# A transformer block pair on one core: the tokens of a batch dealt to four tiles in turn

## The chip, the cores and the metric

One core of a Trainium2 chip runs the whole kernel; the other seven are idle. The core has TensorE (matmuls into PSUM, and their weight loads), VectorE, ScalarE and GpSimd, which read and write SBUF with 128 partitions, and DMA queues. The metric is device time in microseconds of one execution.

## The reference

`x` has 8 batches (B) of 512 tokens (S) with 256 features (D). Two layers follow each other, each adding its result to `x`:

```
x = x + bitlinear(gelu(bitlinear(adapter(x, language))))       # layer 0
x = x + bitlinear(silu(conv3(bitlinear(subject_linear(x)))))   # layer 1

adapter:        h = x + relu(x @ W1[id] + b1[id]) @ W2[id] + b2[id]; layer norm, gamma[id], beta[id]
subject_linear: x @ W[id].T + bias[id]
bitlinear:      weights rounded to -1, 0, 1 times one scale;
                each token rounded to 8 bits by its own largest absolute value; matmul (256 -> 1024 or back)
conv3:          per channel (1024), 3 taps along the 512 tokens of a batch, zero at both ends
```

Everything but `conv3` treats each token by itself. `conv3` needs the tokens of a batch side by side, in their order.

## The kernel before

A batch has TB = 4 tiles of P = 128 tokens. In token layout a partition holds one token of each tile: `xs`, the running value of `x`, keeps on partition p the tokens p, 128 + p, 256 + p and 384 + p, each with 256 features (1 KB). In channel layout a partition is a feature, and the 512 tokens lie along it.

Every engine has one queue with a written order. In `first()` single steps are listed by hand (layer 0 for all batches and the start of layer 1), then `slot2(s)` runs for s = 3 to 8 with the steps of several batches interleaved, then `ending()`. Engines wait for one another through semaphores. A slot of layer 1 moves one batch on by one stage.

The steps that matter here:

- `load_first_tokens` and `load_tokens` (ScalarE's queue) load `xs` of a batch through `x_tiles`; `store2` (SyncE's queue) stores one tile of the result through `out_tiles`.
- `adapter_out(b, p)` (TensorE, L1310): for two tiles, `hT`, the hidden values of the adapter in channel layout, is the stationary operand, 128 tokens at a time; `cw2` is the moving one. It leaves token layout in PSUM.
- `transpose_x` (L1379), `linear` (L1401, L1404) bring a batch through the subject's matrix; `absmax_y`, `scale_y`, `inverse_y` (VectorE) and `round_y` (ScalarE, L619) round it; `transpose_y` (L1416) brings it to channel layout in PSUM, and `lead_q` (ScalarE, L626) copies it into `yT`, bf16, [128, 2, 512].
- `spread_scales` (L1424) and `lead_scales` (ScalarE, L636): the scale of each token, spread to all partitions, is copied from PSUM into `dqb`, [128, 512] fp32.
- `up(b, f)` (L1437): the block f of 128 hidden channels, two matmuls with ternary weights stationary and the 512 columns of `yT` moving. A batch has 8 of them, all batches 64.
- `dequant` (VectorE, L1113) multiplies by `dqb` into `apad`; `last_tap` (ScalarE, L645), `first_tap` (VectorE, L1120), `middle_tap` (GpSimd, L886) and `tap_sum` (GpSimd, L893) make the convolution in `conv`, which is kept in the memory `raw_all`.
- `transpose_conv(b, k)` (L1458): eight transposes of 128 tokens by 128 channels back to token layout. The data are the stationary operand, an identity the moving one. `silu` (ScalarE, L656), the rounding (`round2`), a DMA transpose and `down2` (L1481, L1482) follow.

Of the kernel before, what the change touches and what calls it, by code (L numbers as in the profile page):

```python
# [7 lines left out]
ACT = mybir.ActivationFunctionType  # L8
# [7 lines left out]
P = 128  # L16
# [12 lines left out]
def build_program(nc, t):  # L29
    B, S, D = t["x"].shape  # L30
# [4 lines left out]
    KD = D // P  # L35
    KH = H // P
    TB = S // P
# [6 lines left out]
    with ExitStack() as ctx:  # L44
        def sb(name, shape, dt=F32):
            return ctx.enter_context(nc.sbuf_tensor(name, shape, dt))

        def sem(name):
            return ctx.enter_context(nc.semaphore(name))
# [4 lines left out]
        def wait(eng, s, n):  # L54

            if isinstance(n, int) and n <= 0:
                return
            eng.wait_ge(s, n)
# [3 lines left out]
        def bank(k, n=1):  # L62
            return psum[:, k, :] if n == 1 else psum[:, k:k + n, :]
# [5 lines left out]
        id32 = sb("id32", [P, P])  # L69
# [31 lines left out]
        cw2 = [sb(f"cw2_{k}", [A + 1, D]) for k in range(2)]  # L101
# [5 lines left out]
        dqb = [sb(f"dqb{k}", [P, S]) for k in range(2)]  # L107
        mid_all = [sb(f"mid{k}", [P, 2 * S + 1]) for k in range(2)]
        hT = sb("hT", [A + 1, S])
# [43 lines left out]
        def bank_adapted(b, p):  # L153
            if b == 0:
                return BANK_UP + p
            if b == 1 and p == 1:
                return BANK_UP + 2
            return BANK_AD
# [85 lines left out]
        yT = [sb(f"yT{k}", [P, KD, S], BF16) for k in range(2)]  # L244

        apad = sb("apad", [P, KH, SP2])
        conv = [raw_all[:, 2 * k:2 * k + 2, :].rearrange("p a (f s) -> p (a f) s", s=S) for k in range(2)]
# [17 lines left out]
        def bank_c(b, k):  # L265
            return 3 if b == B - 1 and k % 2 == 1 else 5
# [8 lines left out]
        def bank_x(b):  # L275
            return 0
# [26 lines left out]
        p_bce = sem("p_bce")  # L303
# [44 lines left out]
        def tile(b, j):  # L348
            return TB * b + j + 1

        def pair(b, p):
            return PAIR * b + p + 1
# [9 lines left out]
                slot2(s)  # L362
            ending()

        x_tiles = t["x"].rearrange("b (t p) d -> b p t d", p=P)
        xT_tiles = t["xT"].rearrange("(k p) (b s) -> b p k s", p=P, b=B)
        cw1_all = t["cw1"].rearrange("l (k p) a -> l p k a", p=P)
        out_tiles = t["out"].rearrange("b (t p) d -> b t p d", p=P)
        wl_all = t["cwl1"].rearrange("l (k p) o -> l p k o", p=P)

        block = ctx.enter_context(nc.Block())
# [114 lines left out]
        def _(act):  # L486
# [142 lines left out]
            def lead_scales(b):  # L629
                act.wait_ge(p_bc, b + 1)  # L630
                if b == 0:

                    act.wait_ge(s_zg, PAIRS)
                    act.wait_ge(s_ssq, PAIRS)
                wait(act, p_a, KH * (b - 1))
                act.activation(dqb[b % 2][:, :], bank(bank_x(b)), ACT.Copy).then_inc(p_bce, 1)  # L636

            def last_tap(b, f):

# [46 lines left out]
            def slot2(s):  # L686
                on(last_tap, s - 1, 2)
                on(last_tap, s - 1, 3)
                on(silu, s - 2, 0)
                on(last_tap, s - 1, 4)  # L690
                on(round2, s - 3, 3)
                on(last_tap, s - 1, 5)
                on(silu, s - 2, 1)
                on(dequant2, s - 3, 1)
                on(round_y, s, 0)
                on(round_y, s, 1)
                on(last_tap, s - 1, 6)
                on(round2, s - 2, 0)
                on(lead_scales, s)
                on(last_tap, s - 1, 7)  # L700
                on(silu, s - 2, 2)
                on(lead_q, s)
                on(lead, s + 1, 0)
                on(round2, s - 2, 1)
                on(last_tap, s, 0)
                on(silu, s - 2, 3)
                on(dequant2, s - 3, 3)
                on(lead, s + 1, 1)
                on(last_tap, s, 1)


            def first():
# [20 lines left out]
                dequant_down1(4, 1); round_z(7, 0); gelu(6, 1); gelu(6, 2); untranspose_z(7, 0); gelu(6, 3)  # L733
                round_z(7, 1); dequant_down1(5, 0); gelu(7, 0); dequant_down1(5, 1); untranspose_z(7, 1); gelu(7, 1)
                round_y(0, 0); round_y(0, 1); gelu(7, 2); lead_scales(0); lead_q(0); lead(1, 0); last_tap(0, 0)
                last_tap(0, 1); last_tap(0, 2); lead(1, 1); dequant_down1(6, 0); last_tap(0, 3); last_tap(0, 4)
                last_tap(0, 5); round_y(1, 0); round_y(1, 1); gelu(7, 3); dequant_down1(6, 1); lead_scales(1)
                lead_q(1); last_tap(0, 6); lead(2, 0); last_tap(0, 7); last_tap(1, 0); last_tap(1, 1); lead(2, 1)
                last_tap(1, 2); last_tap(1, 3); silu(0, 0); round_y(2, 0); round_y(2, 1); last_tap(1, 4)
# [508 lines left out]
        def _(pe):  # L1248
# [53 lines left out]
            def adapter_out(b, p):  # L1302
                par = b % 2
                pe.wait_ge(s_relu, b + 1)
                pe.wait_ge(s_ldw2[par], 32 * (b // 2 + 1))
                if b >= 2:
                    wait(pe, s_xx, pair(b, p - 1))
                for k in range(2):
                    c = (2 * p + k) * P
                    ins = pe.matmul(bank(bank_adapted(b, p))[:, k * D:(k + 1) * D], hT[:, c:c + P], cw2[par][:, :],  # L1310
                                    start=True, stop=True)
                ins.then_inc(s_admm, 1)

# [114 lines left out]
            def up(b, f):  # L1428
                if b == 0 and f == 0:

                    pe.wait_ge(s_gelu, tile(B - 1, TB - 2))
                    pe.wait_ge(s_tern[2], 1)
                pe.wait_ge(p_yTe, b + 1)
                g = KH * b + f
                wait(pe, p_first, g - 2)
                for k in range(KD):
                    ins = pe.matmul(bank(BANK_U[g % 3]), w_up1[:, k, f * P:(f + 1) * P],  # L1437
                                    yT[b % 2][:, k, :], start=(k == 0), stop=(k == KD - 1))
                ins.then_inc(p_up, 1)

            def transpose_conv(b, k):
                if k == 0:
                    pe.wait_ge(p_sum, TB * b + TB)
                    if b == 0:
                        pe.wait_ge(s_gelu, tile(B - 1, TB - 1))
                if b < B - 1:
                    if k == 0:
                        wait(pe, p_silu[TB - 1], b)
                    else:
                        pe.wait_ge(p_silu[k - 1], b + 1)  # L1450
                elif k == 0:
                    pe.wait_ge(p_silu[TB - 1], b)
                elif k == 1:
                    pe.wait_ge(p_first, KH * B)
                else:
                    pe.wait_ge(p_silu[k - 2], b + 1)
                for f in range(KH):
                    ins = pe.transpose(bank(bank_c(b, k) + f // KT)[:, (f % KT) * P:(f % KT + 1) * P],  # L1458
                                       conv[b % 2][:, f, k * P:(k + 1) * P], id32[:, :])
                ins.then_inc(p_cT[k], 1)  # L1460

            def down2(b, k):
# [43 lines left out]
            def slot2(s):  # L1506
                on(down2, s - 3, 1)
                on(transpose_conv, s - 2, 2)
                on(up, s - 1, 7)
                on(transpose_y, s)  # L1510
                on(spread_scales, s)
                on(down2, s - 3, 2)
                on(transpose_x, s + 1, 0)
                on(down2, s - 3, 3)
                on(transpose_conv, s - 2, 3)
                on(up, s, 0)
                on(up, s, 1)
                on(transpose_x, s + 1, 1)
                on(up, s, 2)
                on(linear, s + 1, 0)  # L1520
                on(up, s, 3)
                on(down2, s - 2, 0)
                on(transpose_conv, s - 1, 0)
                on(up, s, 4)
                on(linear, s + 1, 1)
                on(up, s, 5)
                on(up, s, 6)
                on(transpose_conv, s - 1, 1)
# [84 lines left out]
```

## Time and profile before

| | us |
|---|---|
| median of 2 runs | 306.22 (305.35 to 307.08) |
| profiled execution, its own time | 302.91 |
| span of the profiled execution | 300.4 |
| granted TensorE clock, mean | 0.98 |

The span runs from the first to the last instruction; 2.5 us of the profiled execution's time lie around it. Busy times are those of the engine's records. A matmul's record holds its way through the array, so that records of neighbours overlap; how closely they follow each other is read from the chain of waits or from the starts in the timeline.

### The profile page before, as it was taken

What the parts mean: (1) busy time and instruction counts of PE and PEld (TensorE: products, weight loads), DVE (VectorE), ACT (ScalarE), POOL (GpSimd) and SP (SyncE); (2) the same over time, 40 slices, a digit from 0 to 9 for tenths busy, and PEclk for the clock granted to TensorE, in tenths of its full rate; (3) what the DMA queues carried; (4) which work ended last, traced back from release to release, by engine and by line L of the source; (5) the groups of instructions that cost most, each with busy time, mean ns of one, the idle gap of its engine ahead of it and who ended that gap; (6) DMA issues with size and microseconds to landing.
All of it is one profiled execution on the core that took longest, in us unless ns stands there. A gap on an engine that the chain in (4) does not pass through costs nothing.

```text
span 300.4 us, 6735 instructions
## 1 busy us (share of the span) xinstructions
PE 268.8 (89%) x1854; PEld 194.0 (65%) x1854; DVE 255.3 (85%) x625; ACT 247.5 (82%) x416; POOL 265.7 (88%) x390
## 2 busy tenths in 40 slices
PE   7698789999989999999998998989989999866794
PEld 7575446566666566666656676767767677635693
DVE  0379899989897999678899999999999999999681
ACT  1759999989899889487769969979799897979752
POOL 2398989889899799999998989999999999999972
PEclk9777999999999999999999999999999999999998
DMA  5896856676675332661122314233394232343575
GB/s 177 304 354 194 275 150 150 157 137 163 158 197 87 72 84 59 130 149 31 24 59 71 70 37 104 40 71 85 29 175 116 53 89 79 100 105 72 136 190 183
DMA packets 87047, 36.92 MB, mean 123 GB/s; under 512 B 71334, under 2 KB 84442, under 8 KB 87011
## 3 DMA queue, kind: packets, MB, share of 16 engines
q1 hardware_dynamic: 80560, 28.40, 40.4%
q10 hardware_dynamic: 6450, 8.10, 8.4%
q8 instruction: 15, 0.25, 0.4%
q14 instruction: 22, 0.17, 0.2%
HBM read 16.04 MB, written 4.19 MB: 67 GB/s over the span
## 4 chain that ended last, share of the span: by engine, by line
PE 42%; ACT 17%; issue 17%; POOL 12%; DVE 4%; DMA 4%; SPq 3%; ACTq 1%; POOLq 0%; DVEq 0%
PE banks L1401 8%; PE banks L1343 5%; PE banks L1362 5%; PE banks L1481 5%; PE banks L1437 4%; PE banks L1458 4%; POOL raw_all L893 3%; DMA raw_all<-in_w2a 3%; ACT ry L619 3%; PE banks L1344 2%; PE banks L1379 2%; ACT g L656 2%; POOL mid L886 2%; POOL r L832 2%; ACT g L592 2%
## 5 line engine op out<-in xcount | busy, mean ns | idle before, releaser
L893 POOL TENSOR_TENSOR raw_all<-raw_all,mid 128x1024 f32<-128x1024 f32 x32 | 63.6, 1996 | 0.0
L645 ACT ACTIVATE banks<-apad,taps 128x512 f32<-128x512 f32 x64 | 44.2, 703 | 15.6 <-DVE apad L1113 15.6
L886 POOL TENSOR_SCALAR mid<-apad,taps,convb 128x512 f32<-128x512 f32 x64 | 48.7, 768 | 0.0
L1120 DVE SCALAR_TENSOR_TENSOR raw_all<-apad,taps,banks 128x512 f32<-128x512 f32 x64 | 46.0, 738 | 1.2 <-ACT banks L645 1.1
L1064 DVE TENSOR_REDUCE am<-g 128x1 f32<-128x1024 f32 x32 | 38.8, 1214 | 7.5 <-ACT g L592 7.2
L1113 DVE TENSOR_TENSOR apad<-banks,dqb 128x512 f32<-128x512 f32 x64 | 43.0, 684 | 2.2 <-PE banks L1437 1.6
L592 ACT ACTIVATE g<-banks,dqz 128x1024 f32<-128x1024 f32 x32 | 35.6, 1117 | 6.9 <-PE banks L1344 4.8
L1343 PE MATMUL banks<-tern,qT 128*128 128x512 bf16 x128 | 38.1, 379 | 2.7 <-ACT qcT L584 2.7
L832 POOL TENSOR_SCALAR r<-g,qs 128x1024 uint16<-128x1024 f32 x32 | 35.8, 1118 | 2.9 <-DVE qs L1076 2.6
L1437 PE MATMUL banks<-yT,tern 128*128 128x512 bf16 x128 | 35.4, 379 | 2.7 <-DVE raw_all L1120 2.5
L1458 PE MATMUL banks<-id,raw_all 128*128 128x128 f32 x256 | 33.6, 275 | 4.6 <-ACT g L656 4.3
L1126 DVE TENSOR_REDUCE am<-g 128x1 f32<-128x1024 f32 x30 | 36.3, 1209 | 0.6 <-ACT g L656 0.6
L1458 PEld LDWEIGHTS banks<-id,raw_all 128*128 128x128 f32 x256 | 28.5, 141 | 9.4 <-ACT g L656 6.8
L1362 PE MATMUL banks<-tern,q1T 128*128 128x256 bf16 x256 | 33.2, 272 | 1.1 <-ACT down L605 0.6
L1401 PE MATMUL banks<-wl,x2T 128*128 128x256 f32 x128 | 32.8, 385 | 1.4 <-issue 1.4
L1481 PE MATMUL banks<-tern,q1T 128*128 128x256 bf16 x240 | 31.2, 273 | 3.0 <-DVE xs L1144 1.5
L656 ACT ACTIVATE g<-banks 128x1024 f32<-128x1024 f32 x30 | 30.7, 1026 | 1.8 <-PE banks L1458 1.8
L1362 PEld LDWEIGHTS banks<-tern,q1T 128*128 128x128 f16 x256 | 24.3, 98 | 8.6 <-issue 3.0
L1481 PEld LDWEIGHTS banks<-tern,q1T 128*128 128x128 f16 x240 | 22.9, 98 | 8.2 <-DVE xs L1144 2.0
L1401 PEld LDWEIGHTS banks<-wl,x2T 128*128 128x128 f32 x128 | 22.0, 190 | 9.3 <-issue 5.4
L663 ACT ACTIVATE r<-g,qs 128x1024 uint16<-128x1024 f32 x21 | 24.6, 1169 | 1.4 <-DVE qs L1139 1.3
L1344 PE MATMUL banks<-bias9b,qcT 128*128 128x512 bf16 x64 | 24.2, 379 | 0.0
(139 smaller groups left out, 599.3 us busy)
## 6 DMA issues: line engine op xcount, KB each, us to landing
out_y<-xs SPq DMA_DIRECT2D x32, 128.0 KB, 2.0
xs<-in_x ACTq DMA_DIRECT2D x7, 512.0 KB, 4.2
x2T<-in_xT ACTq DMA_DIRECT2D x4, 512.0 KB, 5.1
wl<-in_cwl SPq DMA_DIRECT2D x8, 256.0 KB, 2.8
xT<-in_xT ACTq DMA_DIRECT2D x3, 512.0 KB, 4.3
cw<-in_cw SPq DMA_DIRECT2D x16, 64.0 KB, 2.9
raw_all<-in_w1a SPq DMA_DIRECT2D x1, 1024.0 KB, 5.0
raw_all<-in_w2a SPq DMA_DIRECT2D x1, 1024.0 KB, 9.8
```

The lines of the kernel that those rows point to most:

```text
L645: act.activation(bank(BANK_U[g % 3]), apad[:, f, 2:S + 2], ACT.Copy, scale=taps[:, f, 2:3]).then_inc(p_last, 1)
L832: pool.tensor_scalar(r1[j][:, :], g1[j % 2][:, :], qs1[j % 2][:, 0:1], CODE, ALU.mult, ALU.add) \
L886: pool.tensor_scalar(mid[f // 2 % 2][:, f % 2, :], apad[:, f, 1:S + 1], taps[:, f, 1:2], convb[:, f:f + 1], ALU.mult, ALU.add).then_inc(p_ ...
L893: pool.tensor_tensor(c[:, 2 * q:2 * q + 2, :], c[:, 2 * q:2 * q + 2, :], mid[q % 2][:, :, :], ALU.add).then_inc(p_sum, 1)
L1113: dve.tensor_tensor(apad[:, f, 1:S + 1], bank(BANK_U[(KH * b + f) % 3]), dqb[b % 2][:, :], ALU.mult) \
L1120: dve.scalar_tensor_tensor(out=conv[b % 2][:, f, :], in0=apad[:, f, 0:S], scalar=taps[:, f, 0:1], in1=bank(BANK_U[(KH * b + f) % 3]), op0= ...
L1343: pe.matmul(o, qT[p][:, k, c, :], w_up0[:, c, m * 512:(m + 1) * 512], start=(c == 0), stop=False)
L1362: pe.matmul(o, q1T[j][:, c, :].bitcast(F16), w_dn0[:, c, :], start=(c == 0), stop=False)
L1401: pe.matmul(bank(bank_y(b, k))[:, a * D:(a + 1) * D], x2T[:, 2 * k + a, j, :], wl1[par][:, j, :], start=(j == 0), stop=False)
L1437: ins = pe.matmul(bank(BANK_U[g % 3]), w_up1[:, k, f * P:(f + 1) * P], yT[b % 2][:, k, :], start=(k == 0), stop=(k == KD - 1))
L1458: ins = pe.transpose(bank(bank_c(b, k) + f // KT)[:, (f % KT) * P:(f % KT + 1) * P], conv[b % 2][:, f, k * P:(k + 1) * P], id32[:, :])
L1481: pe.matmul(o, q2T[k][:, f, :].bitcast(F16), w_dn1[:, f, :], start=(f == 0), stop=False)
```

## The change

The tokens of a batch are dealt to the four tiles in turn: tile t holds tokens 4p + t, p being the partition. A partition of `xs` then holds the four tokens 4p to 4p + 3, which lie side by side in the tensor in memory (4 KB). In channel layout the tokens keep their order, so at each crossing between the layouts one side counts with a step: `lead_scales` writes `dqb` with a step of 4 elements, `adapter_out` reads `hT` and `transpose_conv` reads `conv` with a step of 4 elements, and `up` reads `yT`, which is still ordered tile by tile, with jumps of 128 elements. The number of instructions, their sizes, their order and their waits are those of before.

```diff
--- before.py
+++ after.py
@@ -362,10 +362,10 @@
                 slot2(s)
             ending()
 
-        x_tiles = t["x"].rearrange("b (t p) d -> b p t d", p=P)
+        x_tiles = t["x"].rearrange("b (p t) d -> b p t d", p=P)
         xT_tiles = t["xT"].rearrange("(k p) (b s) -> b p k s", p=P, b=B)
         cw1_all = t["cw1"].rearrange("l (k p) a -> l p k a", p=P)
-        out_tiles = t["out"].rearrange("b (t p) d -> b t p d", p=P)
+        out_tiles = t["out"].rearrange("b (p t) d -> b t p d", p=P)
         wl_all = t["cwl1"].rearrange("l (k p) o -> l p k o", p=P)
 
         block = ctx.enter_context(nc.Block())
@@ -633,7 +633,8 @@
                     act.wait_ge(s_zg, PAIRS)
                     act.wait_ge(s_ssq, PAIRS)
                 wait(act, p_a, KH * (b - 1))
-                act.activation(dqb[b % 2][:, :], bank(bank_x(b)), ACT.Copy).then_inc(p_bce, 1)
+                act.activation(dqb[b % 2][:, :].rearrange("p (c t) -> p t c", t=TB),
+                               bank(bank_x(b)).rearrange("p (t c) -> p t c", t=TB), ACT.Copy).then_inc(p_bce, 1)
 
             def last_tap(b, f):
 
@@ -1306,8 +1307,7 @@
                 if b >= 2:
                     wait(pe, s_xx, pair(b, p - 1))
                 for k in range(2):
-                    c = (2 * p + k) * P
-                    ins = pe.matmul(bank(bank_adapted(b, p))[:, k * D:(k + 1) * D], hT[:, c:c + P], cw2[par][:, :],
+                    ins = pe.matmul(bank(bank_adapted(b, p))[:, k * D:(k + 1) * D], hT[:, 2 * p + k:S:TB], cw2[par][:, :],
                                     start=True, stop=True)
                 ins.then_inc(s_admm, 1)
 
@@ -1435,7 +1435,8 @@
                 wait(pe, p_first, g - 2)
                 for k in range(KD):
                     ins = pe.matmul(bank(BANK_U[g % 3]), w_up1[:, k, f * P:(f + 1) * P],
-                                    yT[b % 2][:, k, :], start=(k == 0), stop=(k == KD - 1))
+                                    yT[b % 2][:, k, :].rearrange("p (t c) -> p c t", t=TB), start=(k == 0),
+                                    stop=(k == KD - 1))
                 ins.then_inc(p_up, 1)
 
             def transpose_conv(b, k):
@@ -1456,7 +1457,7 @@
                     pe.wait_ge(p_silu[k - 2], b + 1)
                 for f in range(KH):
                     ins = pe.transpose(bank(bank_c(b, k) + f // KT)[:, (f % KT) * P:(f % KT + 1) * P],
-                                       conv[b % 2][:, f, k * P:(k + 1) * P], id32[:, :])
+                                       conv[b % 2][:, f, k:S:TB], id32[:, :])
                 ins.then_inc(p_cT[k], 1)
 
             def down2(b, k):
```

## Rows read from the trace of the kernel before

**Rows 1.** The page, busy time of each engine.
```profile
PE 268.8 (89%) x1854; PEld 194.0 (65%) x1854; DVE 255.3 (85%) x625; ACT 247.5 (82%) x416; POOL 265.7 (88%) x390
```

**Rows 2.** Windows: busy us of each engine, granted clock, DMA share, GB/s.
```profile
160.00:180.00 20.00, 18.64 (x135) 14.34 (x135) 19.16 (x39) 17.35 (x27) 19.08 (x21) 1.00 0.28 64
...
222.00:240.50 18.50, 17.50 (x127) 13.24 (x125) 17.86 (x38) 16.61 (x26) 18.50 (x23) 1.00 0.43 86
...
259.00:282.00 23.00, 16.30 (x122) 11.48 (x119) 21.95 (x43) 18.97 (x25) 22.37 (x23) 1.00 0.43 107
```

**Rows 3.** Chain of waits, 184.9 to 258.2 us: shares, then pieces (start, us, what).
```profile
by line: PE banks L1401 20.3%; PE banks L1481 14.4%; PE banks L1437 12.3%; issue 11.4%; PE banks L1458 9.7%; ACT ry L619 6.1%; PE banks L1379 5.8%; ACT g L656 3.4%; DVE apad L1113 3.0%; POOL raw_all L893 2.7%; PE banks L1416 2.5%; PE banks 
...
224.96 0.89 PE banks L1458 x8
225.85 0.86 PE banks L1437 x4
...
227.15 0.43 PE banks L1437 x2
227.58 0.86 PE banks L1401 x4
...
231.82 0.52 PE banks L1437 x2
```

**Rows 4.** Timeline of TensorE in one slot (start, us).
```profile
225.69 1.03 PE L1437 MATMUL banks<-yT,tern 128*128 128x512 bf16 x4
...
234.56 1.03 PE L1437 MATMUL banks<-yT,tern 128*128 128x512 bf16 x4
...
239.68 0.61 PE L1416 MATMUL banks<-id,ry 128*128 128x128 f16 x8 [0.39 <-ACT ry L619]
```

**Rows 5.** Timeline of VectorE in the same slot.
```profile
234.76 0.69 DVE L1093 TENSOR_REDUCE amy<-banks 128x2 f32<-128x512 f32 x1 [0.20 <-PE banks L1404]
235.37 0.68 DVE L1113 TENSOR_TENSOR apad<-banks,dqb 128x512 f32<-128x512 f32 x1
```

**Rows 6.** Groups of instructions, each shape apart: busy us, mean ns, idle before.
```profile
L1437 PE MATMUL banks<-yT,tern 128*128 128x512 bf16 x128 | 35.4, 379 | 2.7 <-DVE raw_all L1120 2.5
L1401 PE MATMUL banks<-wl,x2T 128*128 128x256 f32 x128 | 32.8, 385 | 1.4 <-issue 1.4
...
L1458 PEld LDWEIGHTS banks<-id,raw_all 128*128 128x128 f32 x256 | 28.5, 141 | 9.4 <-ACT g L656 6.8
...
L1310 PE MATMUL banks<-cw,hT 65*128 65x256 f32 x64 | 17.1, 393 | 1.7 <-ACT hT L556 1.1 <-DVE xx L1020 0.6
...
L1437 PEld LDWEIGHTS banks<-yT,tern 128*128 128x128 bf16 x128 | 11.4, 97 | 12.0 <-issue 5.5
L1310 PEld LDWEIGHTS banks<-cw,hT 65*128 65x128 f32 x64 | 11.3, 195 | 4.0 <-ACT hT L556 1.9 <-issue 0.8
...
L1416 PEld LDWEIGHTS banks<-id,ry 128*128 128x128 f16 x64 | 3.8, 97 | 5.3 <-ACT ry L619 4.3 <-issue 1.0
...
L636 ACT ACTIVATE dqb<-banks 128x512 f32<-128x512 f32 x8 | 5.0, 630 | 0.0
```

**Rows 7.** Timeline of ScalarE in the same slot.
```profile
222.56 0.62 ACT L636 ACTIVATE dqb<-banks 128x512 f32<-128x512 f32 x1
...
224.55 1.07 ACT L626 ACTIVATE yT<-banks 128x1024 bf16<-128x1024 f16 x1
```

**Rows 8.** Chain of waits of the whole span, shares by line.
```profile
by line: issue 16.6%; PE banks L1401 8.0%; PE banks L1343 5.1%; PE banks L1362 4.9%; PE banks L1481 4.7%; PE banks L1437 4.1%; PE banks L1458 3.6%; POOL raw_all L893 3.3%; DMA raw_all<-in_w2a 3.3%; ACT ry L619 2.6%; PE banks L1344 2.4%; PE 
```

**Rows 9.** Chain of waits, 258.2 us to the end, shares by line.
```profile
by line: issue 31.7%; POOL raw_all L893 19.0%; POOL mid L886 12.2%; PE banks L1458 8.8%; PE banks L1481 8.3%; PE banks L1504 4.2%; POOL xs L911 3.5%; POOLq L44 1.8%; POOL raw_all L906 1.6%; POOL dq L875 1.5%; PE banks L1482 1.1%; DVE qs L11
```

**Rows 10.** Timeline of TensorE in the last slot.
```profile
266.29 0.59 PE L1437 MATMUL banks<-yT,tern 128*128 128x512 bf16 x2 [2.16 <-DVE raw_all L1120]
```

**Rows 11.** Chain of waits at the start.
```profile
11.70 9.85 DMA raw_all<-in_w2a
```

**Rows 12.** Windows at the start.
```profile
15.00:20.00 5.00, 5.00 (x30) 3.84 (x30) 2.87 (x2) 3.22 (x6) 4.83 (x5) 0.65 1.07 347
```

## The prediction

> **What bounds the kernel now.** I read four views in this order. The page's first section says that nothing is idle: TensorE is busy 89% of the span and the other three engines 82 to 88% [rows 1]. That alone decides nothing. The windows of one batch of the second layer come next. From 184 to 258 us the kernel repeats itself every 18.5 us; in such a stretch TensorE shows 17.50 us busy, VectorE 17.86, ScalarE 16.61, GpSimd 18.50 [rows 2]. Third is the chain of waits over these four batches: TensorE's lines hold most of it, L1401, L1481, L1437, L1458, L1379 and L1416 alone 65%, and the changed matmul L1437 has 12.3% of 73.3 us, that is 9.0 us, or 21 of the 32 calls of `up` in it, each being two matmuls of 0.216 us [rows 3]. So the order of TensorE's work sets the pace here, up to the second `linear` of a slot; then the chain goes over VectorE (`absmax_y`, `dequant`, `scale_y`) and ScalarE (`round_y`) back to TensorE's `transpose_y`. Fourth is the timeline of TensorE in one slot: its gaps are small, the one ahead of `transpose_y` being 0.39 us [rows 4]. Before 184 us the two layers overlap and the chain changes hands; after 258 us it runs over GpSimd, and TensorE has gaps such as 2.16 us [rows 9, 10].
>
> **What the change does to the instructions.** The order on every engine stays as it is, the waits too. Nothing is added or removed; six access patterns change, so the whole cost lies in how long the same instructions take.
>
> The *moving operand of `up`* (128 matmuls) is the large item. Each reads 512 bf16 columns of `yT`, now one after the other in memory, then in jumps of 128 elements (256 bytes), and back after four. The price when contiguous: four matmuls in 0.86 us, 0.216 us each [rows 3], or 2.4 columns per ns. No row shows a moving operand with a jump. The nearest: the fp32 matmul of `linear` streams 256 columns of 4 bytes, again 0.86 us for four on the chain, its single record 385 ns against the 379 ns of 512 bf16 columns [rows 3, 6]. Both move 1024 bytes per partition in 0.216 us, one 4-byte word each 0.84 ns. If the fetch is by words, each jumping bf16 column needs a word of its own, 512 words, and the matmul takes 0.43 us. If the array's own arithmetic is what limits the fp32 form, this row says nothing, and the cost is 0. Those are the two ends, 0 and +0.216 us per matmul, with an open end above if consecutive jumps also collide. Reads with a step of 4 bytes exist, the fp16 transposes of `ry`: their weight loads take 97 ns, like the 97 ns of a contiguous bf16 load [rows 6]; but that is 128 columns at some 1.3 per ns, a slower stream, so it doesn't exclude the upper end. I take +0.216 us, because the jump here has only two useful bytes at each place and the stream is the fastest of the kernel.
>
> The Trainium skill, Advanced Engine Details and Errata, Memory Cachelines, speaks against this change too: SBUF is read in lines of 16 bytes, and full speed wants at least two hits on a line. By it `up` gets one hit per line and pays, and so do the three places with a step of 16 bytes; the page has no price. At half rate `up` alone would give the sum below, and all four places rival 2 with the 3.4 us of rival 3 on top, 344 us. The Trainium skill, SBUF — State Buffer, Door 1: The DMA port swizzle, repeats the rule, yet calls steps of up to 4 fp32 elements free, which would leave the other three at nothing. No row of the trace before shows an access of either kind.
>
> Where those 0.43 us per `up` (two matmuls) land:
> - Four regular slots, 184 to 258 us. The chain holds 5 `up` per slot (the pieces of 0.86, 0.43, again 0.43, and 0.52 us) [rows 3]: 5 x 0.43 = 2.15 us. The sixth, `up(s,5)`, comes right behind the second `linear`; `dequant` of it sits on VectorE between `absmax_y` and `scale_y` and starts at 235.37, as soon as the reduction is over [rows 5]. With the matmuls of 234.56 [rows 4] ending 0.43 us later it has to wait some 0.35 us. `up(s,6)` and `up(s-1,7)` go into the idle time that TensorE has before `transpose_y`. Slot: +2.5 us, of which small gaps swallow 0.1; four slots +9.6 us.
> - Before 184 us, batches 0 to 2, 24 calls. The whole chain has 4.1% of 300.4 us on L1437, 12.3 us; less 9.0 us leaves 3.3 us, nearly 8 calls [rows 3, 8], +3.3 us. The other 16 would add 6.9 us to a TensorE that is 18.64 of 20 us busy in such a stretch [rows 2]; I let half of it through, +3.4 us. Together +6.7 us.
> - Batch 7, after 258 us: GpSimd holds the chain, TensorE is busy 16.30 of 23 us and waits 2.16 us for VectorE before one `up` [rows 2, 10]. Cover is enough: +0.5 us for delays passed on. If GpSimd were not last there, these eight would cost 3.4 us.
> - Sum of `up`: +16.8 us.
>
> *`transpose_conv`*: conv is the stationary operand, 256 weight loads of 128 fp32 columns, step 16 bytes instead of 4. A load takes 141 ns as recorded, and eight pairs of load and matmul pass in 0.89 us, 0.11 us each [rows 3, 6], so load and matmul are about even and neither hides a slower partner. Ends: 0, and double the 0.11 us. Each column is still one 4-byte word, the same number of words as before; I take 0.
>
> *`adapter_out`*: hT is stationary, 64 loads of 128 fp32 columns, step 16 bytes. A load records 195 ns, its matmul 393 ns [rows 6]; on the chain four matmuls take 0.86 us, so even a doubled load of 0.21 us would fit under the running matmul of 0.216 us. Only the first of a group can show, 16 x 0.11 = 1.8 us at most. I take 0.
>
> *`lead_scales`*: ScalarE writes `dqb` with a step of 16 bytes, 8 times, 630 ns each [rows 6]. Ends: 0, and 512 elements at half their rate, some +0.43 us. ScalarE is without a gap from there to `lead_q`, whose yT ends at 225.62, and `up(s,0)` starts at 225.69 [rows 4, 7]: a longer write would show in full. One word per element before and after; I take 0, and the cost if that is wrong is 8 x 0.43 = 3.4 us.
>
> *DMA*: a load of `xs` has 128 runs of 4 KB in place of 512 of 1 KB (the first batch comes in two halves, with runs of 2 KB); the stores keep runs of 1 KB, now 4 KB apart. Loads matter only in the first 22 us, where the chain waits 9.85 us for w2a while the DMA engines are full, 347 GB/s [rows 11, 12]. One load of 512 KB shares that time: 1.5 us of traffic. It can save between 0 and 1.5 us; I take 0.3, since at 347 GB/s the short runs lose little. Later loads are not waited for. The last store: 0.
>
> **Sum.** +16.8 - 0.3 = +16.5 us on the profiled execution, 302.91 us (span 300.4, 2.5 us around it), gives 319.4 us. The runs shown have a median of 306.22 us, 3.3 us above the profiled one; on that scale the forecast is 322.7 us, **323 us**. With the covers of the early stretch all holding (-3.4) or all failing (+3.4), and DMA at its ends, the case itself reaches from 317 to 328 us.
>
> **Rivals.**
> 1. *Jumps are free* (not slower): TensorE's fetch of the moving operand is not by the word but keeps 2.4 columns per ns at any address. For it: the equal 0.216 us of the fp32 form may be arithmetic, and the 4-byte step of the fp16 loads costs nothing [rows 6]. Decides from the first `up`: its matmul still records 379 ns. Price 0, DMA -0.3: 306 us, 304.5 to 307.
> 2. *The 16-byte step costs in weight loads as well*: `transpose_conv` goes from 0.11 to 0.21 us a piece. The chain has 9.7% of 73.3 us, 7.1 us, on it in the four slots [rows 3] and some 8.8% of the last 42 us, 3.7 us [rows 9]; doubled, with half again for groups now covered and the early slots, that is +18 us on top: 341 us.
> 3. *ScalarE's write costs* and `up` does not: +3.4 us, 309.5 us.
> 4. *Jumps cost more than half rate*, by repeated hits on the same place of the memory: at a quarter rate each call costs 1.3 us more, 64 x 1.3 = 83 us less cover, 380 us.
>
> **How the numbers follow.** Forecast 0.43, rival 1 0.29, rival 2 0.15, rival 3 0.08, rival 4 0.05. For a range of 8 in 10: from 304 us, which takes in rivals 1 and 3 and the forecast, up to 338 us, where it holds some of rival 2; left out are rival 4, most of rival 2 and a little of the forecast's tails. 2% (6.1 us) is about what a measurement of this kernel tells from no change. Faster by that has no mechanism, since the DMA saves at most 1.5 us: 0.01. Within it: rival 1 and nearly all of rival 3, 0.36. Slower: 0.63.
>
> **What would show it.** In the profile of the changed kernel the matmuls of L1437's successor would record some 590 ns in place of 379, four of them passing in 1.7 us; the distance between two `transpose_y` would be 20.9 us in place of 18.5, with VectorE and GpSimd showing gaps. Weight loads of the conv transposes stay at 141 ns, the write of `dqb` at 630 ns. The prediction is wrong if the record stays at 379 ns (rival 1), and wrong in size if gaps of the early stretch swallow more or less than half.

## The result, and the profile after

The changed kernel takes 399.0 us (398.6 to 399.4, two runs) against 306.2 us before: the ratio is 1.311, 95% interval 1.302 to 1.319. It is 93 us slower; the forecast was 323 us.

The page of the changed kernel, parts 1 and 2 (slices of 9.9 us here), its shares of the chain, and three of its costliest groups:

```profile
PE 370.5 (94%) x1841; PEld 220.0 (56%) x1854; DVE 260.1 (66%) x625; ACT 254.5 (64%) x416; POOL 266.9 (67%) x390
...
PEclk9686999999999986798889989999989969886999
...
PE 78%; ACT 10%; issue 5%; DMA 2%; DVE 2%; SPq 1%; ACTq 1%; POOL 0%; POOLq 0%; DVEq 0%
...
L1437 PE MATMUL banks<-yT,tern 128*128 128x512 bf16 x128 | 117.7, 1036 | 2.5 <-DVE raw_all L1121 2.1
L1114 DVE TENSOR_TENSOR apad<-banks,dqb 128x512 f32<-128x512 f32 x64 | 44.3, 691 | 73.8 <-PE banks L1437 73.8
...
L1459 PEld LDWEIGHTS banks<-id,raw_all 128*128 128x128 f32 x256 | 36.4, 210 | 16.1 <-issue 13.0
```

The chain's shares before:

```profile
PE 42%; ACT 17%; issue 17%; POOL 12%; DVE 4%; DMA 4%; SPq 3%; ACTq 1%; POOLq 0%; DVEq 0%
```

TensorE goes from 89% to 94% of a longer span, while the others fall from over 80% to 64 to 67%: they wait for it, as VectorE does, 73.8 us ahead of `dequant` (L1114 here). It has 78% of the chain, where it had 42%. L1437 stands for the moving read of `up`, the same line number by chance. It records 1036 ns where it recorded 379 [rows 6]. The granted clock (PEclk), which before was at 9 tenths in every slice from the fifth to the last but one, now has slices at 6, 7 and 8 tenths in the middle of the run.

The groups of the other three places (busy us, mean ns of one):

```profile
L1310 PEld LDWEIGHTS banks<-cw,hT 65*128 65x128 f32 x64 | 16.3, 325 | 2.8 <-ACT hT L556 2.0 <-issue 0.5
L1310 PE MATMUL banks<-cw,hT 65*128 65x256 f32 x64 | 20.2, 443 | 1.4 <-ACT hT L556 1.1 <-DVE xx L1021 0.3
...
L636 ACT ACTIVATE dqb<-banks 128x512 f32<-128x512 f32 x8 | 9.0, 1127 | 4.9 <-PE banks L1424 4.9
...
L1401 PE MATMUL banks<-wl,x2T 128*128 128x256 f32 x128 | 42.6, 471 | 0.0
```

The weight loads of conv take 210 ns in place of 141, those of hT 325 in place of 195, and the write of `dqb` 1127 in place of 630 [rows 6]: each record of a step of 16 bytes is longer. Whether that costs time is another question, answered below. And L1401, which the change doesn't touch, records 471 ns in place of 385.

The chain of waits in one slot of the changed kernel (start, us, what); it answers to the pieces in [rows 3]:

```profile
253.94 0.45 PE banks L1416 x8
...
254.86 1.13 ACT dqb L636
...
257.74 0.96 PE banks L1459 x8
258.69 3.46 PE banks L1437 x4
...
264.31 0.87 PE banks L1401 x4
...
282.08 0.45 PE banks L1416 x8
```

Four matmuls of `up` pass in 3.46 us, 0.865 us each, against 0.216 before. From one `transpose_y` to the next it is 28.1 us in this slot, the shortest of four (the others take 29.5 to 31.3), against 18.5 before. Every `up` of this slot is now in the chain (16 matmuls), and so is the write of `dqb`, for which `transpose_x` waits.

The first `up` calls of the kernel are the six matmuls from 142.3 us. Windows of the stretch ahead of them, of them, and of the `linear` behind them (us; busy times of TensorE, its weight loads, VectorE, ScalarE, GpSimd; granted clock; DMA share; GB/s):

```profile
139.00:142.00 3.00, 3.00 (x31) 2.44 (x29) 1.78 (x3) 3.00 (x4) 2.92 (x3) 1.00 0.41 93
142.30:147.40 5.10, 5.10 (x6) 0.75 (x7) 1.44 (x3) 1.78 (x3) 2.25 (x4) 0.79 0.00 0
148.30:151.80 3.50, 3.50 (x10) 2.47 (x10) 2.08 (x5) 1.57 (x3) 3.28 (x4) 0.50 0.32 73
```

The clock stands at full rate ahead of them, falls while the jumping reads run, and is at 0.50, that is 1.2 GHz, behind them, although TensorE is busy in the whole of all three windows. The timeline of TensorE has four matmuls of `linear` there; the first line is of the changed kernel, the second of a regular slot before:

```profile
148.27 1.91 PE L1401 MATMUL banks<-wl,x2T 128*128 128x256 f32 x4
```

```profile
227.42 1.03 PE L1401 MATMUL banks<-wl,x2T 128*128 128x256 f32 x4
```

### The profile page after: what moved, and what is told of

The parts are those of the page before. It is cut to its first block, busy times and chain, and to the rows that moved or that the text cites. A ratio compares the mean times of both kernels' runs of the same rounds, so it can differ in the third digit from the quotient of the medians.

```text
span 395.9 us, 6722 instructions
## 1 busy us (share of the span) xinstructions
PE 370.5 (94%) x1841; PEld 220.0 (56%) x1854; DVE 260.1 (66%) x625; ACT 254.5 (64%) x416; POOL 266.9 (67%) x390
## 4 chain that ended last, share of the span: by engine, by line
PE 78%; ACT 10%; issue 5%; DMA 2%; DVE 2%; SPq 1%; ACTq 1%; POOL 0%; POOLq 0%; DVEq 0%
PE banks L1437 28%; PE banks L1401 9%; PE banks L1459 8%; PE banks L1343 6%; PE banks L1362 5%; PE banks L1482 5%; PE banks L1344 3%; PE banks L1310 3%; PE banks L1379 2%; DMA raw_all<-in_w1a 2%; ACT g L592 2%; PE banks L1299 1%; ACT dqb L636 1%; PE banks L1256 1%; ACT squares L568 1%
## 5 line engine op out<-in xcount | busy, mean ns | idle before, releaser
L1437 PE MATMUL banks<-yT,tern 128*128 128x512 bf16 x128 | 117.7, 1036 | 2.5 <-DVE raw_all L1121 2.1
L1114 DVE TENSOR_TENSOR apad<-banks,dqb 128x512 f32<-128x512 f32 x64 | 44.3, 691 | 73.8 <-PE banks L1437 73.8
L1459 PEld LDWEIGHTS banks<-id,raw_all 128*128 128x128 f32 x256 | 36.4, 210 | 16.1 <-issue 13.0
L657 ACT ACTIVATE g<-banks 128x1024 f32<-128x1024 f32 x30 | 30.5, 1021 | 22.2 <-PE banks L1459 22.2
L833 POOL TENSOR_SCALAR r<-g,qs 128x1024 uint16<-128x1024 f32 x32 | 35.7, 1118 | 10.3 <-DVE qs L1077 9.9
L1401 PE MATMUL banks<-wl,x2T 128*128 128x256 f32 x128 | 42.6, 471 | 0.0
L1401 PEld LDWEIGHTS banks<-wl,x2T 128*128 128x128 f32 x128 | 29.2, 244 | 21.8 <-issue 17.3
L1459 PE MATMUL banks<-id,raw_all 128*128 128x128 f32 x256 | 39.4, 302 | 0.4
L1343 PE MATMUL banks<-tern,qT 128*128 128x512 bf16 x115 | 36.0, 386 | 3.4 <-ACT qcT L584 2.5
L1482 PE MATMUL banks<-tern,q1T 128*128 128x256 bf16 x240 | 32.9, 282 | 3.0 <-DVE xs L1145 1.5
L1362 PE MATMUL banks<-tern,q1T 128*128 128x256 bf16 x256 | 34.4, 279 | 0.6 <-ACT down L605 0.3
L1482 PEld LDWEIGHTS banks<-tern,q1T 128*128 128x128 f16 x240 | 24.3, 102 | 18.8 <-issue 12.0
L1437 PEld LDWEIGHTS banks<-yT,tern 128*128 128x128 bf16 x128 | 13.5, 107 | 37.4 <-issue 34.9
L1362 PEld LDWEIGHTS banks<-tern,q1T 128*128 128x128 f16 x256 | 25.1, 101 | 9.7 <-issue 3.8
L902 POOL TENSOR_SCALAR r<-g,qs 128x1024 uint16<-128x1024 f32 x9 | 10.0, 1115 | 27.9 <-DVE qs L1140 27.9
```

What stands on the lines that cost most here:

```text
L1114: dve.tensor_tensor(apad[:, f, 1:S + 1], bank(BANK_U[(KH * b + f) % 3]), dqb[b % 2][:, :], ALU.mult) \
L1343: pe.matmul(o, qT[p][:, k, c, :], w_up0[:, c, m * 512:(m + 1) * 512], start=(c == 0), stop=False)
L1362: pe.matmul(o, q1T[j][:, c, :].bitcast(F16), w_dn0[:, c, :], start=(c == 0), stop=False)
L1401: pe.matmul(bank(bank_y(b, k))[:, a * D:(a + 1) * D], x2T[:, 2 * k + a, j, :], wl1[par][:, j, :], start=(j == 0), stop=False)
L1482: pe.matmul(o, q2T[k][:, f, :].bitcast(F16), w_dn1[:, f, :], start=(f == 0), stop=False)
```

## The experiments

All times are medians. A kernel's change is given by its ratio to runs of the kernel before that were taken on the same chip. Code cuts are shortened where they have dots.

**The jumps alone, put into the kernel before.**

```diff
-                                    yT[b % 2][:, k, :], start=(k == 0), stop=(k == KD - 1))
+                                    yT[b % 2][:, k, :].rearrange("p (t c) -> p c t", t=TB), ...
```

> The kernel before with one edit: `up` reads yT in jumps of 128 elements (its columns come in another order, so the output is not the reference's). Theory A, the moving read alone is the cause: its matmuls record about 1040 ns as in the changed kernel and the time is 385 to 395 us, at least 80 of the 93 us. Theory B, several places share the loss: under 375 us.

388.4 us against 306.4, ratio 1.269 (1.259 to 1.279): +82 us, so theory A holds: the moving read of `up` alone makes most of the loss. Its matmuls record 1040 ns (median), as in the changed kernel.

**The jumps alone, taken out of the changed kernel.**

> The changed kernel with `up` reading yT in order again (the order of its columns no longer fits the scales, so the output is not the reference's). The other three strided places and the DMA runs stay. Theory A: 308 to 316 us, the copy of dqb at 1117 ns giving 3 to 4 us, weight loads at 210 and 325 ns giving 1 to 5 us. Theory B: above 320 us.

> The changed kernel with `up` reading in order, once more with more rounds, since the first measurement was spread from 307.4 to 313.4 us. The sum of the other places done alone should equal it: 309 to 314 us if they add, less if they cover one another.

The first time 312.8 us, spread from 307.4 to 313.4 us, so that it gave no interval; again 312.0 us against 305.3, ratio 1.023 (1.019 to 1.028), that is +7.1 us. Both directions agree: `up` is 82 to 86 of the 93 us, all the other places together 7 to 11.

**TensorE held equally long, without jumps.**

```diff
-                for k in range(KD):
+                for k in [k for _ in range(4) for k in range(KD)]:
                     ins = pe.matmul(bank(BANK_U[g % 3]), w_up1[:, k, f * P:(f + 1) * P],
```

> The kernel before with each pair of matmuls of `up` issued four times (same result, only the last pair counts), all reads in order: TensorE is held for the same 1.73 us per `up` as with jumps, but the array streams columns at full rate. If holding TensorE is all that matters, the time is that of the jumps alone within 2% (385 to 395 us). If the slow stream also lowers the granted clock (0.91 in the changed kernel against 0.98 before), the clock here stays at 0.97 or more and the time is 5 to 12 us under that of the jumps alone.

372.3 us, ratio 1.219 (1.209 to 1.230): +67 us, 16 us under the jumps, where I had expected 5 to 12. Each `up` holds TensorE for 8 x 0.216 = 1.73 us here, and for 2 x 0.865 = 1.73 us with jumps. Windows of the kernel with the jumps alone, then of this one (columns as above):

```profile
139.00:160.00 21.00, 21.00 (x53) 9.45 (x51) 9.22 (x23) 6.07 (x11) 10.24 (x13) 0.67 0.06 13
180.00:200.00 20.00, 19.34 (x78) 8.65 (x77) 11.69 (x24) 12.03 (x18) 15.65 (x16) 0.91 0.22 53
```

```profile
139.00:160.00 21.00, 20.97 (x120) 12.59 (x118) 12.49 (x26) 9.38 (x17) 14.44 (x16) 1.00 0.17 29
180.00:200.00 20.00, 20.00 (x130) 13.62 (x129) 13.23 (x22) 11.10 (x17) 13.16 (x15) 1.00 0.17 38
```

TensorE is busy for 19.34 us or more of each window, and in the first for 21.00 of 21.00 with jumps, yet only with jumps does the granted clock fall, to 0.67 and 0.91. So the stream that passes a column in 1.7 ns did not keep the clock at 2.4 GHz, and the full one did.

That this is what the 16 us are can be seen from whole slots, from one `transpose_y` to the next. Two of the kernel with the jumps alone, then one of this kernel:

```profile
278.67:306.24 27.57, 27.30 (x126) 13.77 (x125) 18.48 (x37) 17.07 (x26) 17.64 (x20) 1.00 0.23 58
306.24:336.51 30.27, 30.13 (x125) 15.88 (x124) 18.48 (x37) 16.75 (x25) 17.63 (x20) 0.89 0.21 53
```

```profile
264.75:292.31 27.56, 27.28 (x173) 18.21 (x172) 18.48 (x37) 17.04 (x26) 17.63 (x20) 1.00 0.23 59
```

In the slot in which the clock stayed at 1.00 the jumps cost what the fourfold stream costs, 27.57 against 27.56 us. Slots at 0.94 take 28.39 and 29.20 us, the one at 0.89 takes 30.27. Who pays is seen in a line that reads alike in both, first with jumps, then without:

```profile
L1401 PE MATMUL banks<-wl,x2T 128*128 128x256 f32 x128 | 42.2, 468 | 0.0
```

```profile
L1401 PE MATMUL banks<-wl,x2T 128*128 128x256 f32 x128 | 32.0, 380 | 0.0
```

That line's records hold 10.2 us more, those of the conv transposes 3.4 us and those of `down2` 1.9 us. Records of neighbours overlap, so this sum only tells where the 16 us lie; the slots tell that the clock is behind them. The jumping matmul itself takes no longer at the lower clock. All its records in the changed kernel (ns, min/median/max):

```profile
L1437 PE MATMUL banks<-yT,tern x128: 1021/1040/1050, 142.3 to 369.9; 128*128 128x512 bf16 x128
```

**The price of each access.** One kernel with eight ways to read `yT`, four ways to read `conv`, four to write `dqb` (one run, 340.8 us; only records are read from it). The part for `up`, abridged, a remark standing for lines of the same form:

```diff
-                                    yT[b % 2][:, k, :], ...
+                    if f == 0: ins = pe.matmul(u, wk, y, **kw)
+                    if f == 1: ins = pe.matmul(u, wk, y.rearrange('p (c t) -> p t c', t=2), **kw)    # 2: t=4, 3: t=8, 4: t=32
+                    if f == 5: ins = pe.matmul(u, wk, y.rearrange('p (t c) -> p c t', t=TB), **kw)
+                    if f == 6: ins = pe.matmul(u, wk, y.rearrange('p (t c d) -> p c t d', t=TB, d=2), **kw)    # 7: d=4
```

> The kernel before with a different access in every block, to read prices from single records (columns are misplaced, so the output is not the reference's). `up` block 0: in order; 1, 2, 3, 4: the same 512 columns with a step of 2, 4, 8, 32 elements (4, 8, 16, 64 bytes); 5: jumps of 256 bytes; 6 and 7: pairs and fours of neighbours between such jumps. `transpose_conv` k = 0..3: step 1, 2, 3, 4 fp32 elements. `lead_scales` b mod 4: step 1, 2, 4, 16 fp32 elements. Theory of lines (16 bytes): blocks 1 and 2 record 379 ns, 3, 4 and 5 alike at about 1040, 6 about 590 or less, 7 about 379; conv steps 1 to 2 at 141 ns, 3 and 4 longer. Theory of colliding jumps: blocks 3 and 4 well under 1040 ns, only the 256-byte jump at 1040, and 6 and 7 at half and a quarter of its excess. For dqb: step 16 like step 4 (1117 ns) if lines decide, more if distance does.

Durations of single records of `up`, ns as min/median/max, blocks 0 to 7 in this order: in order; steps of 4, 8, 16, 64 bytes; jumps of 256 bytes; pairs; fours.

```profile
L1449 PE MATMUL banks<-yT,tern x16: 377/379/389, 138.7 to 298.9; 128*128 128x512 bf16 x16
L1451 PE MATMUL banks<-yT,tern x16: 385/388/392, 139.1 to 299.3; 128*128 128x512 bf16 x16
L1453 PE MATMUL banks<-yT,tern x16: 610/622/640, 139.6 to 300.0; 128*128 128x512 bf16 x16
L1455 PE MATMUL banks<-yT,tern x16: 1059/1078/1080, 142.9 to 303.2; 128*128 128x512 bf16 x16
L1457 PE MATMUL banks<-yT,tern x16: 1017/1033/1035, 144.6 to 306.8; 128*128 128x512 bf16 x16
L1459 PE MATMUL banks<-yT,tern x16: 1022/1042/1048, 146.4 to 308.5; 128*128 128x512 bf16 x16
L1461 PE MATMUL banks<-yT,tern x16: 595/615/618, 154.0 to 309.8; 128*128 128x512 bf16 x16
L1463 PE MATMUL banks<-yT,tern x16: 382/384/401, 154.8 to 313.7; 128*128 128x512 bf16 x16
```

What counts is how many columns each 16-byte line of memory gives before the read leaves it. Eight or four columns a line (in order, step 4, fours): 379 to 388 ns. Two (step 8, pairs): 622 and 615. One (steps 16 and 64, jumps): 1078, 1033, 1042. Distance plays next to no part, 1078 ns at 16 bytes and 1033 at 64. Nor is it the shape of the access pattern: the step of 4 bytes has the pattern of the step of 16, with other numbers, and records 388 ns. A record's excess over 379 ns is 0.66 us for 512 lines; with 0.865 us for 512 lines on the chain, a line costs 1.7 ns at a matmul that takes one column from each, in which the full stream passes four columns. By that price, 256 lines with two columns each take 0.43 us, 128 lines with four 0.22. The theory of colliding jumps falls with the first row of 16 bytes. My expectation for the step of 8 bytes, 379 ns, falls as well: two columns a line are not enough here. Those for pairs (about 590 ns) and fours (about 379) held within 5%.

The weight loads of the conv transposes, steps of 1, 2, 3 and 4 fp32 elements:

```profile
L1486 PEld LDWEIGHTS banks<-id,raw_all x64: 138/141/226, 167.8 to 321.2; 128*128 128x128 f32 x64
L1488 PEld LDWEIGHTS banks<-id,raw_all x64: 194/207/214, 170.8 to 322.2; 128*128 128x128 f32 x64
L1490 PEld LDWEIGHTS banks<-id,raw_all x64: 188/196/213, 175.9 to 325.0; 128*128 128x128 f32 x64
L1492 PEld LDWEIGHTS banks<-id,raw_all x64: 195/209/220, 181.0 to 326.9; 128*128 128x128 f32 x64
```

The step of 2 had been expected at 141 ns. A load is slower from the first step on, about 1.6 ns a column, and no slower at 16 bytes than at 8; here it isn't lines that count. The write of `dqb`, steps of 1, 2, 4 and 16 fp32 elements:

```profile
L638 ACT ACTIVATE dqb<-banks x2: 617/638/660, 137.0 to 225.8; 128x512 f32<-128x512 f32 x2
L640 ACT ACTIVATE dqb<-banks x2: 655/658/661, 156.4 to 248.8; 128x512 f32<-128x512 f32 x2
L642 ACT ACTIVATE dqb<-banks x2: 1130/1156/1183, 175.9 to 271.7; 128x512 f32<-128x512 f32 x2
L644 ACT ACTIVATE dqb<-banks x2: 1052/1053/1054, 202.6 to 295.1; 128x512 f32<-128x512 f32 x2
```

ScalarE writes two fp32 elements a line for nearly nothing, and one a line costs 0.42 to 0.52 us for 512, near or far (two records of each, out of PSUM).

**The price that the prediction assumed.** `up` with a step of 8 bytes, which records 630 ns (median):

```diff
-                                    yT[b % 2][:, k, :], start=(k == 0), stop=(k == KD - 1))
+                                    yT[b % 2][:, k, :].rearrange("p (c t) -> p t c", t=4), ...
```

> The kernel before with `up` reading yT with a step of 4 elements (8 bytes; columns come in another order, so the output is not the reference's). This is the price that the prediction assumed, 0.45 us a matmul in place of 0.216. If the prediction placed it rightly, the time is 321 to 325 us (+16.8, +18 at 0.45 us). Rival, covers were overestimated: above 328 us; or the clock falls here too (mean under 0.96), with 5 us more.

323.6 us, ratio 1.059 (1.053 to 1.065): +18 us, as expected. Two of its starts of `transpose_y` (timeline):

```profile
214.95 0.61 PE L1416 MATMUL banks<-id,ry 128*128 128x128 f16 x8
...
236.10 0.61 PE L1416 MATMUL banks<-id,ry 128*128 128x128 f16 x8
```

A slot of 21.15 us; the prediction had 20.9. From the first `transpose_y` to the one at 184 us this kernel loses 6.4 us (6.7 forecast), in the four slots behind it 10.5 us (9.6), and behind the last `transpose_y` it takes 45.2 us against 42.2 before and 42.7 in two of the runs below, 2.5 to 3 us more (0.5 forecast, with 3.4 named as the price if GpSimd did not cover the last batch); a part of it may be the clock, 0.94 there against 0.96 to 0.98. At the assumed price the sum and most of its covers were right; the cover of the last batch was taken too large. The clock, whose fall had been a rival here, stays up; the granted clock by slices:

```profile
PEclk9667899999999999999999999999999999979998
```

**The other places, one by one.**

```diff
-        x_tiles = t["x"].rearrange("b (t p) d -> b p t d", p=P)
+        x_tiles = t["x"].rearrange("b (p t) d -> b p t d", p=P)
-        out_tiles = t["out"].rearrange("b (t p) d -> b t p d", p=P)
+        out_tiles = t["out"].rearrange("b (p t) d -> b t p d", p=P)
```

> The kernel before with the two layouts of memory alone: `x_tiles` and `out_tiles` deal the tokens in turn, nothing else changes (the convolution and the adapter's tiles then take wrong neighbours, so the output is not the reference's). Theory: loads matter only at the start, 304.5 to 306.5 us against 306.4. Rival, the longer runs of 4 KB help or the 4 KB pitch of the stores hurts the whole way: more than 2 us either way.

The two layouts of memory alone: ratio 1.002 (0.997 to 1.006), nothing that can be told from no change, as expected.

```diff
-                act.activation(dqb[b % 2][:, :], bank(bank_x(b)), ACT.Copy).then_inc(p_bce, 1)
+                act.activation(dqb[b % 2][:, :].rearrange("p (c t) -> p t c", t=TB),
+                               bank(bank_x(b)).rearrange("p (t c) -> p t c", t=TB), ACT.Copy).then_inc(p_bce, 1)
```

> The kernel before with the copy into dqb alone writing with a step of 16 bytes (scales land at other tokens, so the output is not the reference's). The copy records 1117 ns in place of 624. If all of it is on the chain: 8 x 0.49 = +3.9 us, 310 us. Rival, it is covered where ScalarE waits anyway: under +1 us.

Ratio 1.014 (1.008 to 1.020), +4.2 us: all of 8 x 0.49 us shows, as expected.

```diff
-                                       conv[b % 2][:, f, k * P:(k + 1) * P], id32[:, :])
+                                       conv[b % 2][:, f, k:S:TB], id32[:, :])
```

> The kernel before with transpose_conv alone reading conv with a step of 16 bytes (tokens are dealt differently from the rest, so the output is not the reference's). Eight transposes take 0.96 us in place of 0.89 (210 ns a weight load, partly hidden): 32 groups x 0.07 = 2.2 us less cover, +1 to +2 us. Rival, a load exposed in full (70 ns each, 256 times, as the start of each group shows): +5 us or more.

Ratio 1.001 (0.997 to 1.005), that is between -1.0 and +1.4 us, at the lower end of the expected +1 to +2. In the profile a slot takes 18.65 us in place of 18.50: loads of 210 ns stay nearly covered.

```diff
-                                       hT[:, c:c + P], cw2[par][:, :],
+                                       hT[:, 2 * p + k:S:TB], cw2[par][:, :],
```

> The kernel before with adapter_out alone reading hT with a step of 16 bytes (tokens are dealt differently from the rest, so the output is not the reference's). Weight loads of 325 ns in place of 190 under matmuls of 0.216 us: 64 x 0.03 to 64 x 0.13 = 2 to 8 us on TensorE, which isn't last for most of layer 0: 0 to +3 us. Rival, they are exposed on the chain: +4 us or more.

Ratio 0.999 (0.995 to 1.003): the loads, 329 ns here, are covered.

These four give +4.6 us together and the changed kernel without the jumps +7.1; each of the five carries over 1 us of uncertainty either way, so that a difference between 4.6 and 7.1 is not shown. The changed kernel has some 10 us beside its `up`. Its slot with the clock at 1.00:

```profile
253.76:281.90 28.14, 27.69 (x126) 14.22 (x124) 18.48 (x37) 17.49 (x26) 17.65 (x20) 1.00 0.28 66
```

That is 0.57 us more than the 27.57 us of the jumps alone, or 4.6 us in eight slots, which the dearer write of `dqb` (0.49) and the conv transposes account for. The other slots stand at 0.94 and 0.84, and the mean clock is 0.906 to 0.912 against 0.925 to 0.933 with the jumps alone; that the remaining 5 us or so go with the clock fits this, but no run separates them.

**The order restored earlier.** Two versions that compute the reference with the new layout of memory and read `yT` in order. In the first, `lead_q` puts the columns of `yT` in the order of the tokens (only its edit is shown):

```diff
-                act.activation(yT[b % 2][:, :, :], bank16(bank_y(b, 0), F16).rearrange("p (k s) -> p k s", k=KD),
-                               ACT.Copy, bias=-OFFSET).then_inc(p_yTe, 1)
+                act.activation(yT[b % 2][:, :, :].rearrange("p k (c t) -> p k t c", t=TB),
+                               bank16(bank_y(b, 0), F16).rearrange("p (k t c) -> p k t c", k=KD, t=TB),
+                               ACT.Copy, bias=-OFFSET).then_inc(p_yTe, 1)
```

> The changed kernel, but the order is restored one step earlier: lead_q writes yT with a step of 4 bf16 elements (8 bytes) and `up` reads it in order, so TensorE's fast stream meets no jump. The prices of dqb (step 2 of fp32, 8 bytes, cost 30 ns) say the copy of 1024 elements stays near 1.1 us; the time is then that of the changed kernel with `up` undone, 309 to 314 us. Rival, the copy doubles like the write with a step of 16 bytes: about +1 us for each of 8 batches, 317 to 322 us.

322.0 us, ratio 1.052 (1.046 to 1.057): the expected 309 to 314 us did not come, the rival's 317 to 322 did, at its upper edge. The copy takes 2.5 us in place of 1.07:

```profile
L626 ACT ACTIVATE yT<-banks x8: 2522/2538/2573, 137.1 to 279.0; 128x1024 bf16<-128x1024 f16 x8
```

In the second, the transposes of `spread_scales` reorder the scales besides, so that the copy into `dqb` is in order again:

```diff
-                    ins = pe.transpose(bank(bank_x(b))[:, k * P:(k + 1) * P],
+                    ins = pe.transpose(bank(bank_x(b))[:, k:S:TB],
```

> As the version in which the copy reorders yT, and the scales are reordered one step earlier too: the transposes of spread_scales write PSUM with a step of 4 fp32 elements, and the copy into dqb reads and writes in order (624 ns again). If TensorE writes PSUM with a step at full rate: 3 to 4 us below that version. Rival, the PSUM write with a step costs as much: four transposes of 0.11 us become 0.2 to 0.45 us each, and nothing is won.

318.4 us, ratio 1.045 (1.040 to 1.050), 3.6 us below the first, as expected. Its transposes and its copy of the scales:

```profile
L637 ACT ACTIVATE dqb<-banks 128x512 f32<-128x512 f32 x8 | 5.1, 642 | 0.0
L1424 PE MATMUL banks<-id,dqy 128*128 128x128 f32 x32 | 4.8, 273 | 0.0
```

TensorE writes fp32 into PSUM with a step of 16 bytes at no price, 273 ns as before, and the copy is back at 642 ns. Both versions beat the changed kernel by 77 and 81 us and stay behind the one before. The new layout of memory by itself gained nothing that could be measured, so there was nothing for them to win over it.

## Why the prediction was wrong

**The step that failed** is the price of the moving operand of `up`. The prediction took +0.216 us per matmul, from the row in which 4-byte words and 2-byte columns pass in equal time [rows 3, 6], as if a jump cost a word. With one column from each 16-byte line the read took 1.7 ns a line, so the matmul took 0.865 us and the excess was 0.65 us, three times as much. The same price per line explains half rate with two columns a line. The upper end had been left open and then all but dropped: rival 4, the quarter rate, had a chance of 0.05, and the range ended at 338 us. Nothing in the rows spoke for half rate against quarter rate; the choice went to the end that had a row near it, and the range should have gone to the other. Rival 4 had the right rate by luck: its reason, repeated hits of far jumps on one place, falls with the step of 16 bytes, which records 1078 ns.

One hit on a line is slow in the runs, 1033 to 1078 ns against 379; the Trainium skill, Advanced Engine Details and Errata, Memory Cachelines, had this sign. Where it asks for two hits a line and the runs show 615 to 622 ns at two and 384 to 388 at four, the measurement decides, and likewise where the Trainium skill, SBUF — State Buffer, Door 1: The DMA port swizzle, calls a step of 4 fp32 elements free and the write of `dqb` takes 1117 ns against 624.

**The placing of the sum** was right in the main. At the assumed price 323.6 us came out, for 323 forecast. Five `up` of a slot in the chain, a sixth over VectorE, half of the early ones covered: that fits, with +2.65 us a slot for +2.4. Only behind the last `transpose_y` the profile has 2.5 to 3 us more in place of 0.5. At the true price it no longer holds, since the gaps of a slot are used up and all eight `up` are in the chain: of 64 calls x 1.3 us = 83 us, 67 showed with the clock held.

**Missing altogether** was TensorE's clock. No rival had it. It cost 16 us, the difference between two kernels that hold TensorE equally long. Rival 4, 380 us, came nearest to the 388 us of the jumps alone, but its 83 us less cover were 67 and made 372; the 16 us of the clock, which it had not, brought the time above it.

**`lead_scales`** was taken at 0 and cost 0.49 us a copy; its price if wrong, 3.4 us, and its place, the chain of ScalarE ahead of `lead_q`, were right (4.2 us measured for 3.4). **`transpose_conv`** and **`adapter_out`** were taken at 0: their loads did get slower, by 70 and 130 ns, but neither moved the time of the kernel before. For `adapter_out` the cover was named rightly, the running matmul. For `transpose_conv` the prediction said that nothing hides a slower load, and priced rival 2 at +18 us; that was wrong, loads of 210 ns cost 0.15 us a slot. (Rival 2's own terms, 7.1 and 3.7 us with half again, give +16; and the ends named for the case, added up, give 318 to 326 us, or 329 with the last batch uncovered, for the 317 to 328 stated. Neither slip moves the forecast.) **DMA**: -0.3 us forecast; measured, between -0.8 and +1.8 us. Slower had a chance of 0.63 and came.

## What to carry to other kernels

Before a rearranged read is given to TensorE's moving operand, count the columns that it takes from each 16 bytes: here four or eight bf16 columns cost nothing (379 to 388 ns a matmul), two halved the rate (0.45 us on the chain for 0.216), one quartered it (0.865 us), however near the next line was. Put such a reordering where it was free or nearly so here (a weight load under a matmul, a PSUM write of a transpose), and price it by one run with a different variant in every block before the layout of a whole program is built on it. A price with no row near its upper end needs that end in the range.

## What the runs showed of the hardware that was not expected

- With the moving stream at one column a line the granted clock fell (0.67 in a stretch in which TensorE was busy throughout), while a full stream of equal length kept it at 1.00. At two columns a line it stayed up as well. The jumping matmul itself is no slower at the lower clock, 1021 to 1050 ns in all its 128 records; its neighbours are.
- ScalarE's write of bf16 with a step of 8 bytes costs more than fp32 with a step of 16: 1.47 us more for 1024 elements, 1.4 ns each, against 0.49 us for 512, 1.0 ns each. Fp32 with a step of 8 bytes costs 20 ns in all. Both steps of 8 bytes put two elements on a 16-byte line, so a price by lines does not explain ScalarE's writes; why they differ is open.
- A weight load of 128 fp32 columns takes 207 ns at a step of 8 bytes and 209 at 16, 141 in order.
- TensorE's fp32 transposes write PSUM with a step of 16 bytes in 273 ns, as in order, and the next matmul follows the four of them after 0.44 us in both.
